# A graph layer with attention and experts: waiting aggregates as fp16 pairs, one layer as the loop body, and a reordered opening

## The chip, the core and the metric

The kernel runs on one core of a Trainium2 chip. The metric is the device time of one execution in microseconds (us), the median of several runs. TensorE is PE in the rows, VectorE is DVE, ScalarE is ACT, GpSimd is POOL and SyncE is SP.

## What is computed

The input is a node matrix x of 6250 rows by 512 columns and 100000 edges (src, dst), sorted by dst. After a layer norm of the rows the kernel adds a graph term and an attention term to x, then adds a mixture of two experts to the result.

```python
xn  = layernorm(x)
agg = segment_sum(xn[src], dst, 6250);  ah = agg / max(degree, 1)
gnn = xn @ W1.T + b1 + ah @ W2.T + b2
q, k, v = split(xn @ qkv_w.T); q, k = relu(q), relu(k)      # 16 heads of 32
p   = (q @ (k.T @ v)) / (q @ sum(k) + 1e-15)                # per head
x2  = x + gnn + p @ proj_w.T + proj_b
xn2 = layernorm(x2); pooled = sum(xn2 * softmax(xn2 @ attn_w))
g, (e1, e2) = top-2 gates of softmax(pooled @ gate_w + gate_b)
out = x2 + sum over the two experts of g * gelu(gelu(xn2 @ w1 + b1) @ w2 + b2)
```

## The kernel before, in words

The rows are cut into T = 49 tiles of 128. Precise values are carried as two fp16 halves (high and low), and `three` forms a product of such pairs with 12 matmuls of 128x512: high by high and high by low (L523, L524), then low by high (L526). Each engine has a program of its own, written out in order, and semaphores join them. There is no scheduler: the order in the source is the order on the engine, and a `Fori` is a loop on that engine.

**Pass 1** (iterations i = -1 to 49). ACT and DVE normalize tile n (`normalize(n)`: statistics L1073, L1074, scale L1059 to L1062, values L846 and L851, low half L1068), `LEAD` tiles ahead of PE and three in two iterations by `norm_slots`. SP stores the pair as a row block of `table` in DRAM. PE transposes tile i+1 (L658), which ACT copies into xT (L904), and turns a weight block in most of the early iterations (`prepare`, L569). It then computes the keys of tile i (L523 to L526), which ACT takes twice (L918, L920). The low half is made by POOL until i = KP = 28, afterwards by DVE (L1202), and PE adds the products of keys and rows of tile i-1 into four banks (L678 to L680). The first keys need the key weights: two loads, 16 transposes (L541), the largest entry (L1043), a matmul that spreads it over the partitions (L532), the high half on ACT (L895) and the low half on DVE (L1180).

**Gathers.** Once the table is stored, POOL issues 784 indirect DMAs (L496), each with the rows of 128 edges, into a ring of 16 slots, four slots for each release by PE. SP counts the landings and tells PE. These 784 instructions are written out one by one.

**Aggregates.** For a tile DVE builds one-hot matrices (`match`, L1125, L1131). PE multiplies them with the gathered rows, about 17 blocks in a tile (`agg_first`, `group`, `agg_last`: L583, L584, L586, L609, L639). Only three tiles are aggregated within pass 1 (`EARLY`), and one between the passes. When a tile is done DVE takes the degree and its reciprocal (`degrees`, L1139, L1142), and ACT scales the bank into one of four slots of `ah`, in fp32 (`keep_ah`, L887). There it waits for its layer.

**Pass 2** (`layer(i)`). Layer i computes queries of tile i, turns the aggregate (L735) and the attention input (L742) of tile i-1 and forms their linear products. It also aggregates tile i+skew, and normalizes and turns tile i-2 (L776). The skew is 2, then 1, then 0 (`LAYERS`). Since `ah` is indexed by a Python number k, the loop body holds four layers. The loops run over i = 4 to 15, 20 to 31 and 36 to 47, three turns each. The other layers are written out. After a turned aggregate ACT copies its high half (L954) and DVE makes the low half (L1293).

**Pass 3** computes the two experts in groups of four tiles.

Of the kernel before, what the change touches and what calls it, by code (L numbers as in the profile page):

```python
# [20 lines left out]
P = 128  # L21
# [23 lines left out]
LEAD = 6  # L45
# [63 lines left out]

def layers(eng, body):  # L110
# [12 lines left out]

def program(nc, x, src, dst, gw1, gb1, gw2, gb2, qkv_w, proj_w, proj_b, attn_w, attn_b, gate_w, gate_b,
            w1, b1, w2, b2, out):
    ctx = ExitStack()
    with ctx:
# [11 lines left out]
        def slots(first, n):  # L139
# [42 lines left out]
        k32, khl, kacc = work[:, 4], [work[:, 5 + b].bitcast(F16) for b in range(2)], work[:, 7]  # L182
        x2, xn2, acc, pT_, x_in, w32, xb, ahT_ = (work[:, k] for k in range(8))
        ah = work[:, 8:12]
# [76 lines left out]
        ps_o, ps_b, ps_ta, ps_tp, ps_tx = bank[1], bank[2], bank[3], bank[4], bank[0]  # L261
# [10 lines left out]
            turned_x2 agg_made dg_made rd_made ah_made ahT_hi ahT_lo pT_hi pT_lo lin_made xa_made x2_made x2_stored  # L272
# [16 lines left out]
        def natural(t):  # L289

            if t < T - NS:
                return xT[:, t + OFF].rearrange("p a n -> p (a n)")
            return (work[:, 10], work[:, 11], awb[:, :])[t - (T - NS)].bitcast(F16)
# [20 lines left out]
        def _(sp):  # L314
# [68 lines left out]
            with sp.Fori(0, passes) as a:  # L383
                with sp.Fori(0, ROUNDS) as g:
                    for k in range(R):
                        sp.wait_ge(slot_loaded[k], (a * ROUNDS + g) * 16 + 16)
                        if k % U == U - 1:
                            sp.sem_inc(s["arrived"], 1)
# [53 lines left out]
        def _(pool):  # L442
# [30 lines left out]
            for i in range(KP + 1):  # L473
# [7 lines left out]
                pool.tensor_tensor(out=khl[i % 2][:, D:2 * D], in0=k32, in1=khl[i % 2][:, 0:D],  # L481
# [35 lines left out]
        def _(pe):  # L517
# [132 lines left out]
            pe.sem_inc(s["oh_used"], OG)  # L650
            n = 0
            for i in range(-1, T + 1):
                t = i + 1
                if t < T:
                    pe.wait_ge(s["lo_made"], t + 1)
                    after(pe, s["t_taken"], t)
                    for q in range(2 * C):
                        r = nc.tensor.transpose(ps_t[:, q, :], natural(t)[:, q * P:(q + 1) * P], ident16[:])  # L658
                    r.then_inc(s["t_made"], 1)
# [3 lines left out]
                if 0 <= i < T:  # L663
                    pe.wait_ge(s["t_taken"], i + 1)
                    after(pe, s["k32_made"], i)
                    after(pe, s["khi_made"], i)
                    if i == 0:
                        pe.wait_ge(s["scales_made"], 1)
                        pe.wait_ge(s["wk_hi"], C)
                        pe.wait_ge(s["wk_lo"], C)  # L670
                    three(ps_k[:, :], lambda c: xT[:, i, c, :], lambda c: xT[:, i, C + c, :],
                          lambda c: wk[:, 0, c, :], lambda c: wk[:, 1, c, :], C).then_inc(s["k_made"], 1)
# [161 lines left out]
        def _(act):  # L834
            F = nc.scalar.activation

            for t in range(XI):
                act.dma_start(xin[:, t, :], x[t * P:(t + 1) * P, :]).then_inc(x_loaded[t], 16)
# [649 lines left out]
```

## Time and profile before

| what | value |
|---|---|
| runs, us | 1998.27, 1991.93, 2003.87 (median 1998.27) |
| the profiled execution | 2016.52 us, of which its span is 2013.7 us |
| granted TensorE clock, mean | 0.904 of full speed |
| PE busy | 1672.8 us, 83% of the span |
| DVE busy | 1055.3 us, 52% |
| ACT busy | 642.5 us, 32% |
| POOL busy | 841.4 us, 42% |
| pass 1, pass 2, pass 3 | to about 400 us, 440 to 1700 us, 1760 to 2014 us |

Busy time is the time in which an engine executes; the rest it waits or issues. The granted clock of 1.0 stands for 2.4 GHz and 0.5 for 1.2 GHz. In the rows a matmul's time is the time in which it is under way. Matmuls overlap, so the distance of their starts is what one costs.

### The profile page before, as it was taken

The numbers are of one execution on the slowest core, as the hardware profiler recorded it, in microseconds if no ns is written. First come the engines' busy times: TensorE is split into PE (matmuls) and PEld (weight loads), VectorE is DVE, ScalarE is ACT, GpSimd is POOL, SyncE is SP. The second block draws the span as 40 slices with busy tenths as digits, with TensorE's granted clock in tenths as the row PEclk, the third lists the DMA queues.
The fourth block names the chain that finished last, engine by engine and source line by source line (L and its number), as shares of the span: only waits on it lengthen the run. The fifth ranks groups of instructions, "written<-read, shape, count | busy, mean of one in ns | idle before, by whom it ended". The sixth has DMA issues, their size and how long they took to land.

```text
span 2013.7 us, 31010 instructions
## 1 busy us (share of the span) xinstructions
PE 1672.8 (83%) x8557; PEld 795.2 (39%) x8558; DVE 1055.3 (52%) x2199; ACT 642.5 (32%) x980; POOL 841.4 (42%) x867
## 2 busy tenths in 40 slices
PE   5999887788878878988888877887788878499997
PEld 3554333343434333433343333433334334244443
DVE  8665122144555444654555454744455545467667
ACT  6787322111222212312222221311222212355554
POOL 2444333335555555356555556355555552000000
PEclk9999898989988888988888888988898888699999
DMA  8433322335565565455655556456555553212232
GB/s 282 163 126 110 94 84 84 87 118 166 174 183 171 158 181 174 130 177 179 178 168 165 166 177 183 125 172 185 172 178 162 166 171 107 99 63 104 96 112 93
DMA packets 113596, 296.39 MB, mean 147 GB/s; under 512 B 18602, under 2 KB 21188, under 8 KB 113260
## 3 DMA queue, kind: packets, MB, share of 16 engines
q0 software_dynamic: 62720, 205.57, 35.1%
q1 hardware_dynamic: 35424, 60.21, 8.9%
q10 hardware_dynamic: 15372, 29.58, 4.2%
q8 instruction: 46, 0.75, 0.2%
q14 instruction: 34, 0.28, 0.0%
HBM read 255.80 MB, written 39.49 MB: 147 GB/s over the span
## 4 chain that ended last, share of the span: by engine, by line
PE 68%; issue 16%; DVE 4%; another core or an unknown queue 3%; ACT 2%; DVEq 0%; DMA 0%; ACTq 0%; SPq 0%
PE bank L523 15%; PE bank L524 14%; PE bank L526 14%; PE bank L583 9%; PE bank L584 8%; PE bank L776 1%; PE bank L678 1%; PE bank L679 1%; PE bank L680 1%; PE bank L742 1%; PE bank L735 1%; DVE ring L1432 1%; PE bank L658 0%; PE bank L586 0%
## 5 line engine op out<-in xcount | busy, mean ns | idle before, releaser
L496 POOL DMA_INDIRECT ring<-table,src_col x784 | 758.8, 968 | 710.8 <-PE bank L609 384.9
L583 PE MATMUL bank<-ring,onehot 128*128 x830 | 319.7, 385 | 59.5 <-issue 49.8
L584 PE MATMUL bank<-ring,onehot 128*128 x830 | 322.4, 388 | 43.0 <-issue 42.3
L1139 DVE TENSOR_SCALAR dg<-bank 128x1 f32<-128x1 f32 x49 | 7.7, 158 | 459.5 <-PE bank L639 206.5
L523 PE MATMUL bank<-wts,xT 128*128 128x512 f16 x588 | 229.7, 391 | 14.4 <-ACT work L920 11.2
L887 ACT ACTIVATE work<-bank,rd 128x512 f32<-128x512 f32 x49 | 33.7, 687 | 631.0 <-issue 360.0
L524 PE MATMUL bank<-wts,xT 128*128 128x512 f16 x588 | 229.8, 391 | 0.0
L523 PE MATMUL bank<-wts,work 128*128 128x512 f16 x392 | 181.6, 463 | 26.2 <-issue 25.7
L524 PE MATMUL bank<-wts,work 128*128 128x512 f16 x392 | 181.7, 464 | 14.1 <-issue 13.3
L1131 DVE TENSOR_TENSOR onehot<-iota_t,dst_col 128x512 f32 x244 | 169.0, 693 | 44.9 <-DVE iota_t L1125 24.6
L586 PE MATMUL bank<-ones,onehot 128*128 128x1 f16 x830 | 138.4, 167 | 43.1 <-issue 42.5
L526 PE MATMUL bank<-wts,xT 128*128 128x512 f16 x588 | 153.7, 384 | 1.5 <-issue 1.5
L526 PE MATMUL bank<-wts,work 128*128 128x512 f16 x392 | 119.9, 424 | 29.4 <-issue 29.0
L583 PEld LDWEIGHTS bank<-ring,onehot 128*128 x830 | 80.7, 97 | 152.0 <-issue 73.5
L586 PEld LDWEIGHTS bank<-ones,onehot 128*128 x830 | 80.9, 97 | 148.8 <-issue 62.2
L584 PEld LDWEIGHTS bank<-ring,onehot 128*128 x830 | 80.1, 96 | 63.1 <-issue 54.2
L945 ACT ACTIVATE xT<-bank 128x512 f32 (+1 forms) x49 | 29.2, 597 | 196.4 <-PE bank L776 111.1
L523 PEld LDWEIGHTS bank<-wts,xT 128*128 128x128 f16 (+1 forms) x588 | 58.7, 100 | 79.5 <-issue 22.0
L526 PEld LDWEIGHTS bank<-wts,xT 128*128 128x128 f16 (+1 forms) x588 | 58.5, 100 | 73.3 <-issue 6.6
L1006 ACT ACTIVATE work<-work 128x512 f32<-128x512 f32 x98 | 61.8, 630 | 80.2 <-DVE work L1442 79.1
L481 POOL TENSOR_TENSOR work<-work 128x512 f16<-128x512 f32 x29 | 34.0, 1171 | 127.7 <-ACT work L920 127.7
L524 PEld LDWEIGHTS bank<-wts,xT 128*128 128x128 f16 (+1 forms) x588 | 58.7, 100 | 57.2 <-issue 6.6
(259 smaller groups left out, 2800.2 us busy)
## 6 DMA issues: line engine op xcount, KB each, us to landing
ring<-table,src_col POOLq DMA_INDIRECT x784
x_rows<-work ACTq DMA_DIRECT2D x49, 256.0 KB
work<-in_x ACTq DMA_DIRECT2D x48, 256.0 KB
ring<-x_rows SPq DMA_DIRECT2D x12, 1024.0 KB, 5.3
out_x<-ring SPq DMA_DIRECT2D x12, 1024.0 KB
table<-xT SPq DMA_DIRECT2D x46, 256.0 KB, 2.0
ring<-in_x SPq DMA_DIRECT2D x42, 256.0 KB, 2.7
xT<-in_L_mix_qkv_weight SPq DMA_DIRECT2D x2, 1024.0 KB, 8.9
```

The source lines that it names most:

```text
L481: pool.tensor_tensor(out=khl[i % 2][:, D:2 * D], in0=k32, in1=khl[i % 2][:, 0:D], op=ALU.subtract).then_inc(s["klo_made"], 1)
L496: pool.indirect_dma_start(ring[:, n, :], None, table[:, :], bass.IndirectOffsetOnAxis(ap=ap, axis=0)).then_inc(slot_loaded[n], 16)
L523: mm(out_, wh(c), mh(c), start=first and c == 0, stop=False)
L524: mm(out_, wh(c), ml(c), start=False, stop=False)
L526: r = mm(out_, wl(c), mh(c), start=False, stop=last and c == n - 1)
L583: mm(ps_agg[:, :], w[:, k, :], rows[:, k, 0:D], start=start, stop=False, skip_group_check=True)
L584: r = mm(ps_agg[:, :], w[:, k, :], rows[:, k, D:2 * D], start=False, stop=stop, skip_group_check=True)
L586: d = mm(ps_deg[:, 0:1], w[:, k, :], ones16[:, 0:1], start=start, stop=False, skip_group_check=True)
L887: F(ah[:, k % SLOTS, :], ps_agg[:, :], ACT.Copy, scale=rd[:]).then_inc(s["ah_made"], 1)
L945: F(tile(t)[:, 0:C, :], ps_tx[:, :].rearrange("p (c n) -> p c n", c=C), ACT.Copy).then_inc(s["x2T_hi"], 1)
L1006: F(act2[:, j % 2, e], pre[:, j % 2, e], ACT.Gelu).then_inc(s["act_made"], 1)
L1131: V.tensor_tensor(onehot[:, bass.ds((q + t) % OG * U, U), :], iota_t[:, None, :].to_broadcast([P, U, P]), dst_col[:, bass.ds(q % GROUPS * ...
```

## The change

`ah` becomes a pair of fp16 halves. ACT writes the high half while it scales the bank (`ah_hi`), and DVE writes the low half straight from the bank (`ah_made`), at the end of `degrees`. PE then turns eight fp16 blocks instead of four fp32 blocks, ACT copies the turned pair in one instruction, and the DVE instruction L1293 is gone. The slot is indexed by a register. With that one layer is the body of the loops of pass 2, and they cover i = 4 to 16, 18 to 32 and 34 to 47. From i = 30 on pass 1 becomes loops too (`stretch`, `LATE`), cut where a tile is aggregated, and the first of these aggregates moves from i = 35 to i = 36. The gathers stay written out. In the opening `LEAD` falls from 6 to 3, `norm_slots` gives five tiles in three iterations, ACT issues two loads of x before the first statistics and four after, and DVE measures the key weights after the statistics of one tile.

```diff
-LEAD = 6
+LEAD = 3
-EARLY = {35: 0, 41: 1, 47: 2}
+EARLY = {36: 0, 41: 1, 47: 2}
+LATE = ((30, 37), (37, 42), (42, T - NS - 1))
-LAYERS = ((1, 2, None), (2, 16, 2), (16, 17, None), (17, 32, 1), (32, 33, None), (33, T, 0), (T, T + 3, None))
+LAYERS = ((1, 2, None), (2, 17, 2), (17, 18, None), (18, 33, 1), (33, 34, None), (34, T, 0), (T, T + 3, None))
 def norm_slots(i):
-    n = LEAD + (3 * (i + 1) + 1) // 2
-    return range(n, min(LEAD + (3 * (i + 2) + 1) // 2, T + 2))
+    n, m = (LEAD + (5 * k + 2) // 3 for k in (i + 1, i + 2))
+    return range(n, min(m, T + 2))
 def layers(eng, body):
     for lo, hi, skew in LAYERS:
-        a, b = min(max(-(-lo // SLOTS), 1), hi // SLOTS), hi // SLOTS
-        for i in range(lo, a * SLOTS if b > a else hi):
-            body(i, skew, i % SLOTS)
-        if b > a:
-            with eng.Fori(a, b) as g:
-                for k in range(SLOTS):
-                    body(g * SLOTS + k, skew, k)
-            for i in range(b * SLOTS, hi):
-                body(i, skew, i % SLOTS)
+        a, b = max(lo, 4), min(hi, T - 1)
+        if b - a < 2:
+            a = b = hi
+        for i in range(lo, a):
+            body(i, skew)
+        if a < b:
+            stretch(eng, lambda i: body(i, skew), a, b)
+        for i in range(b, hi):
+            body(i, skew)
...
+            def late(i):
+
+                turn_tile(i + 1)
+                key(i)
+                gram(i - 1)
+            for lo, hi in LATE:
+                stretch(pe, late, lo, hi)
+                if hi - 1 in EARLY:
+                    aggregate(EARLY[hi - 1])
...
-                    for c in range(C):
-                        r = nc.tensor.transpose(ps_ta[:, c * P:(c + 1) * P], ah[:, (k - 1) % SLOTS, c * P:(c + 1) * P], ident[:])
+                    for q in range(2 * C):
+                        r = nc.tensor.transpose(ps_ta[:, q, :], one(ah, t % SLOTS)[:, q * P:(q + 1) * P], ident16[:])
...
-                F(ah[:, k % SLOTS, :], ps_agg[:, :], ACT.Copy, scale=rd[:]).then_inc(s["ah_made"], 1)
+                F(one(ah, t % SLOTS)[:, 0:D], ps_agg[:, :], ACT.Copy, scale=rd[:]).then_inc(s["ah_hi"], 1)
...
             act.wait_ge(s["consts"], 2)
-            for n in range(LEAD - 1):
-                normalize(n)
+            normalize(0)
+            load_x(range(2, XI))
+            normalize(1)
...
                 V.reciprocal(rd[:], dg[:]).then_inc(s["rd_made"], 1)
+                after(dve, s["ah_hi"], t + 1)
+                a2 = one(ah, t % SLOTS)
+                V.scalar_tensor_tensor(out=a2[:, D:2 * D], in0=ps_agg[:, :], scalar=rd[:], in1=a2[:, 0:D],
+                                       op0=ALU.mult, op1=ALU.subtract).then_inc(s["ah_made"], 1)
...
-            for n in range(3):
-                normalize(n)
+            normalize(0)
             for h in range(2):
                 dve.wait_ge(wk_loaded[h], 16)
                 largest(raw_w[WK][:, 2 * h:2 * h + 2], 6 + h)
-                if h == 0:
-                    normalize(3)
...
-                    after(dve, s["ahT_hi"], t + 1)
-                    V.tensor_tensor(ahT[:, 1], ps_ta[:, :].rearrange("p (c n) -> p c n", c=C), ahT[:, 0],
-                                    ALU.subtract).then_inc(s["ahT_lo"], 1)
```

In the opening, ACT's program before had these instructions, from the fourth statistics to the first copied tile:

```order
L856 ACTIVATE std<-mv,epsc 128x1 [waits mv_made]
L846 ACTIVATE ring<-ring,nmr,rstd 128x512 [waits lo_made,nmr_made]
L851 ACTIVATE xT<-ring,nmr,rstd 128x512
L856 ACTIVATE std<-mv,epsc 128x1 [waits mv_made]
L895 ACTIVATE wts<-bank,scale 128x512 [waits wk_turned,scales_made]
L895 ACTIVATE wts<-bank,scale 128x512 [waits wk_turned] x3
L846 ACTIVATE ring<-ring,nmr,rstd 128x512 [waits lo_made,nmr_made]
L851 ACTIVATE xT<-ring,nmr,rstd 128x512
L856 ACTIVATE std<-mv,epsc 128x1 [waits mv_made]
L904 ACTIVATE xT<-bank 128x1024 [waits t_made]
```

Now it has these, from behind the first two loads to the same copy:

```order
L900 ACT_TABLE_LOAD [waits mv_made]
L900 ACTIVATE std<-mv,epsc 128x1 [waits consts]
L881 DMA ring<-in_x 128x512 x4
L890 ACTIVATE ring<-ring,nmr,rstd 128x512 [waits nmr_made]
L895 ACTIVATE xT<-ring,nmr,rstd 128x512
L900 ACTIVATE std<-mv,epsc 128x1 [waits mv_made]
L955 ACTIVATE wts<-bank,scale 128x512 [waits wk_turned,scales_made]
L955 ACTIVATE wts<-bank,scale 128x512 [waits wk_turned] x3
L890 ACTIVATE ring<-ring,nmr,rstd 128x512 [waits nmr_made]
L895 ACTIVATE xT<-ring,nmr,rstd 128x512
L900 ACTIVATE std<-mv,epsc 128x1 [waits mv_made]
L937 ACTIVATE xT<-bank 128x1024 [waits t_made]
```

The four scaled key blocks (`wts<-bank,scale`) stand behind two square roots and one normalized tile. Before, five square roots and four tiles stood ahead of them.

At the end of an aggregate, ahead of the one-hot matrices of the next tile, DVE's program before had these instructions (`first_i` holds the block numbers, which are loaded into registers):

```order
L1139 TENSOR_SCALAR dg<-bank 128x1 [waits agg_made]
L1142 RECIPROCAL rd<-dg 128x1 [waits ah_made,dg_made]
L1123 TENSOR_LOAD first_i
L1123 ISA x2
L1124 TENSOR_LOAD first_i
L1124 ISA x2
L1125 TENSOR_SCALAR iota_t<-iota,tile_base 128x128
```

Now it has these, at the same place:

```order
L1204 TENSOR_SCALAR dg<-bank 128x1 [waits agg_made]
L1207 RECIPROCAL rd<-dg 128x1 [waits ah_made,dg_made]
L1210 SCALAR_TENSOR_TENSOR work<-bank,rd,work 128x512 [waits ah_hi]
L1188 TENSOR_LOAD first_i
L1188 ISA x2
L1189 TENSOR_LOAD first_i
L1189 ISA x2
L1190 TENSOR_SCALAR iota_t<-iota,tile_base 128x128
```

One instruction of 128x512, which waits for ACT, now stands between the reciprocal and the next tile's register loads.

## Rows read from the trace of the kernel before

**Rows 1.** Stages: us, busy time (x instructions) of each engine, granted clock, DMA share, GB/s.

```profile
100.00:150.00 50.00, 49.46 (x300) 26.13 (x299) 34.82 (x89) 41.73 (x71) 22.48 (x18) 1.00 0.39 126
...
1000.00:1200.00 200.00, 161.15 (x812) 74.50 (x812) 98.96 (x214) 43.61 (x64) 113.37 (x118) 0.86 0.58 172
```

**Rows 2.** Timeline of the opening: start us, us, engine, line, what, [idle before <-releaser].

```profile
8.58 3.65 PE L541 MATMUL bank<-ident,xT 128*128 128x128 f32 x16 [4.96 <-DMA xT<-in_L_mix_qkv_weight]
...
18.14 0.77 PE L532 MATMUL bank<-ring,ones 128*128 128x128 f32 x2 [5.92 <-DVEq L1171]
...
21.38 2.42 ACT L895 ACTIVATE wts<-bank,scale 128x512 f16<-128x512 f32 x4 [0.89 <-DVEq L1176]
...
23.44 2.69 DVE L1180 SCALAR_TENSOR_TENSOR wts<-bank,scale,wts 128x512 f16<-128x512 f32 x4
...
25.27 1.03 ACT L904 ACTIVATE xT<-bank 128x1024 f16<-128x1024 f16 x1
...
28.11 0.63 PE L523 MATMUL bank<-wts,xT 128*128 128x512 f16 x1
...
49.82 0.67 PE L532 MATMUL bank<-ring,ones 128*128 128x256 f32 x2 [1.21 <-DVEq L1196]
```

**Rows 3.** Timeline of ACT, three copies of a turned tile in the steady part.

```profile
99.95 1.02 ACT L904 ACTIVATE xT<-bank 128x1024 f16<-128x1024 f16 x1 [1.43 <-PE bank L658]
...
106.43 1.03 ACT L904 ACTIVATE xT<-bank 128x1024 f16<-128x1024 f16 x1
...
112.52 1.02 ACT L904 ACTIVATE xT<-bank 128x1024 f16<-128x1024 f16 x1 [1.43 <-PE bank L658]
```

**Rows 4.** Timeline of pass 1's late part, PE and ACT.

```profile
221.69 0.61 PE L658 MATMUL bank<-ident,xT 128*128 128x128 f16 x8
...
231.88 1.02 ACT L904 ACTIVATE xT<-bank 128x1024 f16<-128x1024 f16 x1 [11.50 <-remote]
...
340.38 1.02 ACT L904 ACTIVATE xT<-bank 128x1024 f16<-128x1024 f16 x1 [8.90 <-remote]
...
400.87 0.60 ACT L918 ACTIVATE work<-bank 128x512 f32<-128x512 f32 x1 [6.72 <-remote]
```

**Rows 5.** Timeline of one layer and the start of the next.

```profile
1005.62 0.16 DVE L1139 TENSOR_SCALAR dg<-bank 128x1 f32<-128x1 f32 x1 [10.85 <-PE bank L639]
...
1006.01 0.69 ACT L887 ACTIVATE work<-bank,rd 128x512 f32<-128x512 f32 x1 [14.18 <-issue]
...
1008.22 2.86 DVE L1131 TENSOR_TENSOR onehot<-iota_t,dst_col 128x512 f32 x4 [0.63 <-DVE iota_t L1125]
...
1013.44 0.60 PE L735 MATMUL bank<-ident,work 128*128 128x128 f32 x4
...
1014.32 0.38 PE L583 MATMUL bank<-ring,onehot 128*128 x1
...
1016.58 0.94 POOL L496 DMA_INDIRECT ring<-table,src_col  x1 [6.86 <-PE bank L609]
...
1028.04 0.38 PE L583 MATMUL bank<-ring,onehot 128*128 x1 [1.02 <-issue]
...
1038.43 0.38 PE L523 MATMUL bank<-wts,xT 128*128 128x512 f16 x1
...
1041.02 0.60 PE L735 MATMUL bank<-ident,work 128*128 128x128 f32 x4
```

**Rows 6.** Timeline of POOL in an earlier layer.

```profile
539.32 0.94 POOL L496 DMA_INDIRECT ring<-table,src_col  x1 [5.38 <-PE bank L609]
...
551.10 0.94 POOL L496 DMA_INDIRECT ring<-table,src_col  x1 [1.91 <-remote]
```

**Rows 7.** Waits of DVE: us in total, times, longest us.

```profile
DVE iota_t L1125 <- issue: 60.3, 44, 1.9
```

**Rows 8.** DMA queues from 620 to 840 us: packets, MB, share of 16 engines.

```profile
q14 instruction: 1, 0.01, 0.0%
```

**Rows 9.** DMA queues from 850 to 1000 us, the same columns.

```profile
q8 instruction: 6, 0.10, 0.3%
```

More of the change, by code:

```diff
@@ L382, in _, with landed @@
             passes = sp.value_load(first_i[0:1, T + 1:T + 2], min_val=1, max_val=T)
[L383 to L388, printed above, removed]
+            def landed(it):
+                for k in range(R):
+                    sp.wait_ge(slot_loaded[k], it * 16 + 16)
+                    if k % U == U - 1:
+                        sp.sem_inc(s["arrived"], 1)
+            with sp.Fori(0, ROUNDS) as g:
+                landed(g)
+            with sp.If(passes > 1):
+                with sp.Fori(1, passes) as a:
+                    with sp.Fori(0, ROUNDS) as g:
+                        landed(a * ROUNDS + g)
             sp.wait_ge(s["chosen"], 1)
@@ L650, in _, with turn_tile, key, gram @@
             pe.sem_inc(s["oh_used"], OG)
-            n = 0
[L652 to L659, printed above, removed]
+            def turn_tile(t):
+                after(pe, s["t_taken"], t)
+                for q in range(2 * C):
+                    r = nc.tensor.transpose(ps_t[:, q, :], natural(t)[:, q * P:(q + 1) * P], ident16[:])
+                r.then_inc(s["t_made"], 1)
+            def key(t):
+                pe.wait_ge(s["t_taken"], t + 1)
+                after(pe, s["k32_made"], t)
+                after(pe, s["khi_made"], t)
+                three(ps_k[:, :], lambda c: tile(t)[:, c, :], lambda c: tile(t)[:, C + c, :],
+                      lambda c: wk[:, 0, c, :], lambda c: wk[:, 1, c, :], C).then_inc(s["k_made"], 1)
+            def gram(t, first=False, last=False):
+                pe.wait_ge(s["klo_made"], t + 1)
+                kh, kl = one(khl, t % 2)[:, 0:D], one(khl, t % 2)[:, D:2 * D]
+                for c in range(C):
+                    xh, xl = natural(t)[:, c * P:(c + 1) * P], natural(t)[:, D + c * P:D + (c + 1) * P]
+                    mm(bank[c][:, :], xh, kh, start=first, stop=False)
+                    mm(bank[c][:, :], xh, kl, start=False, stop=False)
+                    r = mm(bank[c][:, :], xl, kh, start=False, stop=last)
+                r.then_inc(s["g_made"], 1)
+            n = 0
+            for i in range(-1, LATE[0][0]):
+                pe.wait_ge(s["lo_made"], i + 2)
+                turn_tile(i + 1)
                 for kind, c in STEPS.get(i, ()):
@@ L682, in _ @@
+            for i in range(LATE[-1][1], T + 1):
+                if i + 1 < T:
+                    turn_tile(i + 1)
+                if i < T:
+                    key(i)
+                gram(i - 1, last=(i == T))
                 if i in EARLY:
-                    if EARLY[i] == 0:
-                        pe.wait_ge(s["steps_act"], STEPS_ALL)
-                        pe.wait_ge(s["steps_dve"], STEPS_ALL)
-                        pe.wait_ge(s["firsts_made"], 1)
                     aggregate(EARLY[i])
@@ L914, in _, with late @@
                 if i >= 0:
-                    act.wait_ge(s["k_made"], i + 1)
-                    after(act, s["klo_made"], i)
-                    after(act, s["kacc_made"], i)
-                    F(k32, ps_k[:, :], ACT.Relu, scale=SK).then_inc(s["k32_made"], 1)
-                    after(act, s["g_made"], i - 1)
-                    F(khl[i % 2][:, 0:D], ps_k[:, :], ACT.Relu, scale=SK).then_inc(s["khi_made"], 1)
+                    take_key(i)
+            for t in range(T - NS, T):
+                stored(act, t)
+            def late(i):
+                take_tile(i + 1)
+                take_key(i)
+            for lo, hi in LATE:
+                stretch(act, late, lo, hi)
+                if hi - 1 in EARLY:
+                    keep_ah(EARLY[hi - 1])
+            for i in range(LATE[-1][1], T):
+                if i + 1 < T:
+                    take_tile(i + 1)
+                take_key(i)
                 if i in EARLY:
-                    keep_ah(EARLY[i], EARLY[i])
+                    keep_ah(EARLY[i])
             act.wait_ge(s["pt_stored"], 16)
@@ L1176, in _ @@
             dve.sem_inc(s["scales_made"], 1)
[L1177 removed]
+            normalize(2)
             for c in range(C):
```

130 lines of the change are left out of this document (73 added, 57 removed).

## The prediction

> **What bounds the kernel now.** I read the stages first. From 100 to 150 us PE is busy for 49.46 of 50 us at full clock: pass 1 is bound by PE, and what ACT, DVE or POOL do there costs nothing unless PE then waits. From 1000 to 1200 us, in pass 2, PE is busy for 161.15 of 200 us, the granted clock is 0.86 (a mixture of 2.4 and 1.2 GHz), and no other engine is over 60% [rows 1]. So the two stages have different limits, and I read a timeline in each.
>
> Pass 2 takes most of the time. A layer lasts from one turned aggregate at 1013.44 to the next at 1041.02, 27.6 us [rows 5]. POOL starts a burst of gathers at 1016.58. Some 11 us into the burst PE begins to idle between its instructions, with no semaphore to blame: 1.02 us, put down to issue, at 1028.04 [rows 5]. In that stretch it starts about one instruction in 0.7 us for some 7 us, and runs at half clock for about as long after it. In an earlier layer the burst from 539.32 ends before that, and POOL's next one starts at 551.10 after a pause [rows 6]; there the layer lasts 20 us and PE has no such stretch. So a layer's length hangs on how long POOL gathers without a pause, and neither on ACT nor on DVE: ACT was idle for 14.18 us before it scaled the aggregate, DVE for 10.85 us before it took the degree [rows 5].
>
> The same shape shows three times in the late part of pass 1. ACT gets a copy's release late, after 11.50 us of idling at 231.88, 8.90 at 340.38 and 6.72 at 400.87 [rows 4]. The releaser is "remote", and PE had made the tile long before: the first of them ended its transposes at 221.69 + 0.61 = 222.30 [rows 4]. From there to 231.88 are 9.6 us; all three together make 9.6 + 8.9 + 6.7 = 25.2 us in which PE has nothing to do. They too begin some ten us after POOL began an unbroken burst.
>
> **The opening.** Before, the 16 transposes of the key weights are done at 8.58 + 3.65 = 12.23, but the matmul that spreads the largest entry starts only at 18.14, and ACT scales the high half at 21.38, since DVE and ACT normalize tiles in between [rows 2]. Now one tile stands ahead of the measurement on DVE, so PE's matmul can follow its transposes at about 12.3. From 18.14 to 21.38 are 3.24 us, of which DVE spends 0.9 on a tile's statistics; without them the high half starts at about 14.5, 6.9 us earlier. The low half ended at 23.44 + 2.69 = 26.13, 4.75 us after the high half began [rows 2]; a tile's normalization stands between them, for which I allow 0.9 more: 20.1. The first keys followed ACT's copy of tile 0 by 28.11 - 25.27 = 2.84 us [rows 2]. With the copy now behind one tile of ACT's (some 2 us after the high half ends at 16.9) that would give 22; DVE reaches the low half of tile 1 later than it did, so I take 23.5 to 24, a gain of 4.3. It isn't all kept. The matmul for the next scale stands at 49.82, after an idle time of 1.21 that DVE caused [rows 2]. DVE's work ahead of it is the same in sum, so I expect it at 48.9, or 45 if PE alone set it. The gain carried on is 1.4 to 5; I take **-3 us**. Four of the loads of x are issued behind ACT's first square root; a late one would move the second or third tile only.
>
> **The pattern of normalized tiles.** ACT's copies are 106.43 - 99.95 = 6.48 us apart across an iteration with two tiles, and 112.52 - 106.43 = 6.09 across one with one [rows 3]; ahead of the second copy ACT shows no idle time, so there ACT is as late as PE. Now two iterations of three have two tiles, where one of two had. If each added double costs 6.48 - 6.09 = 0.39, the bound is 30/6 x 0.39 = 2 us for the thirty iterations, less what the fewer iterations with norms give back. If ACT fell behind in each of 20 doubles it would be 20 x 0.39 = 8. I take **+1.2 us**: the copy at 106.43 was released without a wait, nearer to the small end.
>
> **The late part as loops.** PE's, ACT's and DVE's instructions are the same, and one aggregate moves from behind i = 35 to behind i = 36. What the loops save is code. Whether the three late releases go with it is a rival below. My value is **0**: they follow POOL's burst, and POOL's gathers stay as they are.
>
> **The layers.** Hidden, each:
> - DVE's new low half: one of 128x512 from a bank, like the one of 23.44 (2.69 / 4 = 0.67 us each [rows 2]), and ahead of it a wait for ACT's 0.69 us [rows 5]. Behind it on DVE stand the next tile's one-hot matrices. They would start at about 1008.22 + 0.9 = 1009.1, and the first four be done by 1012, where PE takes its first block at 1014.32 [rows 5]. The cover is 14.32 - 11.08 = 3.2 us; without it this edit would cost 0.9 us x 46 = 41 us.
> - The removed subtraction on DVE took as long and had the same cover: 0.
> - Eight fp16 transposes took 0.61 us in pass 1 [rows 4], four fp32 ones 0.60 [rows 5]: 0.
> - ACT's copy takes 1.02 us [rows 3] where it took about 0.6, with 14.18 us of idle time to spend [rows 5].
>
> **Loop turns.** There were 9 turns of loops in pass 2 and are 13 + 15 + 14 = 42. One lies ahead of the query at 1038.43, where i passes from 23 to 24, and PE shows no idle time there [rows 5]. DVE shows 60.3 us before L1125 in 44 times, 1.37 on average, and 1.9 at the longest [rows 7]; if the excess of 0.5 is the turn, 33 more cost 33 x 0.5 = 17.5 us on DVE, and nothing on PE as long as the 3.2 us above stand. I take **0**.
>
> **The sum** is -3 + 1.2 + 0 + 0 = -1.8 us. The profiled execution took 2016.52 us, 18 more than the median of 1998.27; a change of this size is carried over as it stands: **1996 us**.
>
> **A rule against the change.** The DMA queues show that code is fetched while the program advances: from 850 to 1000 us, mostly written-out layers, the queue of instructions moved six blocks [rows 9], and from 620 to 840, in the later turns of a loop, one queue moved a single packet and the other none [rows 8]. Layers take 27 to 28 us in both stretches. So neither fetching nor its absence costs anything that I can see. The Trainium skill ("Runtime: NRT & Kernel Launch", section "Instruction fetch mechanics") says that a taken branch whose target lies outside a window of two pages waits for a fetch, and that kernels therefore unroll; its blocks of 16 KiB agree with 0.10 MB for six. By it loops of four layers would pay at each turn and loops of one might not. The trace has no fetch at the turns of either kind of loop to show it.
>
> **Rivals.**
> - *The late releases come from written-out code.* ACT's three late releases lie where PE fetched code; in loops it doesn't. For it: they are put down to "remote", and no engine was busy. Against it: they last 7 to 10 us, the layers show the same in a loop and outside one, and bursts of POOL lead all of them. It gives 1996 - 25 = **1971**. Chance 0.20.
> - *PE's stretch of slow issue in the layers comes from the length of the loop body*, and a body of one layer ends it. A layer would last 20 us as in the stretch of [rows 6], some 7 less, for 46 layers less four that have none: about 1996 - 42 x 7 = **1700**. Against it: written-out layers and loops are alike. Chance 0.03.
> - *Slower: the turn of a loop is exposed on PE's path.* It is DVE's turn that matters: the price is 17.5 us as above if the one-hot matrices arrive late, which needs 3.2 us of delay at the start of a tile where I count 0.9 + 0.5. Layers with a tile of 18 blocks come nearest. It gives 1996 + 17.5 = **2013.5**. Chance 0.17.
> - *My forecast*: 0.60. Its own range is 1988 to 2006: the opening at -5 or -1.4 and the pattern at +8 or 0 give -5 to +6.6, and runs scatter by 6 about their median.
>
> **How the numbers follow.** What a measurement here can tell from no change is about 0.5%, 10 us: faster is under 1988.3, slower over 2008.3. Of my forecast's 0.60, 0.06 lies under the one and 0.03 over the other. Faster is then 0.20 + 0.03 + 0.06 = 0.29. Slower is 0.17, of which 0.02 lies within the bound, and 0.03: 0.18. The rest, 0.53, is the same. The range goes from 1968, under the first rival, to 2016, over the last; only the 1700 is left out, with tails of each.
>
> **What the profile will show.** Right: the first keys at 23.5 to 24, the spreading matmul of the second scale at about 49; in the late part ACT waits three times for 6 to 12 us with "remote" named; layers of 27 to 28 us, PE idle "issue" some 11 us into POOL's burst; clock about 0.86 in the middle of pass 2; DVE's new instruction at 0.67 to 0.75 us and one-hot matrices done over 2 us before their first block. Wrong: a late part without the three waits (first rival); layers of 20 us (second); idle time on PE before a tile's first block that a one-hot matrix ends (third). A cost that I can't see is what a shorter body does to the burst itself: if POOL's gathers are released in another rhythm, each layer's slow stretch could move by more than all terms above.

## The result, and the profile after

The changed kernel took 2032.77 us (median of 4 runs, 2023.00 to 2036.49), the kernel before 1997.84 us (4 runs, 1991.93 to 2003.87). The ratio is 1.0167, with an interval from 1.0119 to 1.0215: slower by 35 us. Forecast were 1996 us and a range up to 2016. The profiled execution of the changed kernel took 2030.38 us. A ratio, here and below, leaves out executions that are over 1.5% above the fastest of their kernel, while a median holds them all (pause_8: 1.0042 by medians, 1.0004 as ratio).

Its stages, with the columns of [rows 1]:

```profile
0.00:25.00 25.00, 11.57 (x68) 8.83 (x69) 20.50 (x62) 13.95 (x23) 4.30 (x23) 0.86 0.81 273
25.00:50.00 25.00, 17.35 (x82) 8.07 (x81) 18.90 (x35) 16.00 (x28) 7.58 (x6) 0.85 0.72 237
50.00:75.00 25.00, 24.77 (x140) 12.66 (x138) 15.39 (x48) 18.61 (x34) 7.60 (x6) 0.94 0.63 187
...
100.00:150.00 50.00, 47.31 (x288) 24.94 (x286) 34.50 (x90) 40.15 (x68) 23.07 (x18) 1.00 0.40 127
1000.00:1200.00 200.00, 162.57 (x853) 75.56 (x854) 104.93 (x221) 47.91 (x67) 112.86 (x117) 0.87 0.58 169
```

Pass 2 reads as before. Pass 1 doesn't: from 100 to 150 us PE is busy for 47.31 us where it was for 49.46 [rows 1], and from 25 to 50 us its granted clock is 0.85 (1.00 before). The timeline of the changed kernel, PE in the opening and ACT in the late part:

```profile
20.82 0.63 PE L538 MATMUL bank<-wts,xT 128*128 128x512 f16 x1
...
29.70 0.58 PE L538 MATMUL bank<-wts,xT 128*128 128x512 f16 x1 [4.44 <-ACT work L946]
...
48.16 0.67 PE L547 MATMUL bank<-ring,ones 128*128 128x256 f32 x2 [3.21 <-DVEq L1271]
...
229.37 0.60 ACT L944 ACTIVATE work<-bank 128x512 f32<-128x512 f32 x1 [4.53 <-remote]
...
240.96 1.02 ACT L937 ACTIVATE xT<-bank 128x1024 f16 x1 [10.51 <-remote]
...
355.05 1.02 ACT L937 ACTIVATE xT<-bank 128x1024 f16 x1 [7.59 <-remote]
...
413.55 0.60 ACT L944 ACTIVATE work<-bank 128x512 f32<-128x512 f32 x1 [6.01 <-remote]
```

The first keys come at 20.82 us, 7.3 us earlier than at 28.11 [rows 2]. The next keys then wait 4.44 us for ACT, and the spreading matmul of the second scale 3.21 us for DVE. The late releases are still there, as before the change [rows 4].

A good ruler is the start of ACT's copy of the keys of tile i (L918 before, L944 after), since it stands once in every iteration, and then the turned aggregate of layers 0 and 48 (L735 before, L776 after). All times are us in the profiled execution:

| kernel | i = 4 | i = 28 | layer 0 | i = 28 to layer 0 | layers 0 to 48 |
|---|---|---|---|---|---|
| before | 59.74 | 208.04 | 441.13 | 233.1 | 1258.4 |
| changed, first profile | 59.23 | 214.24 | 455.99 | 241.7 | 1258.4 |
| changed, second profile | 57.58 | 214.31 | 460.11 | 245.8 | 1272.7 |

By layer 0 the first profile of the changed kernel is 14.9 us behind: 6.2 by i = 28, 8.7 from there on. The layers cost nothing in the first profile and 14 us in the second. One execution of a kernel differs from another by more than the term that was forecast for them. The medians are 35 us apart and these two profiled executions only 14 (2030.38 and 2016.52), since the one of before lies 18 us above its median; the profiles alone don't show where the rest is.

### The profile page after: what moved, and what is told of

Its sections match the earlier page's. It is cut to its first block, busy times and chain, and to the rows that moved or that the text cites. A ratio compares the mean times of both kernels' runs of the same rounds, so it can differ in the third digit from the quotient of the medians.

```text
span 2028.6 us, 33311 instructions
## 1 busy us (share of the span) xinstructions
PE 1688.6 (83%) x8753; PEld 798.8 (39%) x8754; DVE 1060.8 (52%) x2199; ACT 663.9 (33%) x980; POOL 837.9 (41%) x867
## 4 chain that ended last, share of the span: by engine, by line
PE 43%; issue 26%; DVE 9%; DVEq 5%; ACT 5%; another core or an unknown queue 4%; ACTq 1%; DMA 0%; SPq 0%
PE bank L538 10%; PE bank L539 10%; PE bank L541 9%; PE bank L598 5%; PE bank L599 4%; DVEq L1196 1%; PE bank L687 1%; PE bank L689 1%; PE bank L688 1%; ACT work L1019 1%; DVE work L1360 1%; DVE work L1357 1%; DVE st L1363 1%; DVEq L1189 1%
## 5 line engine op out<-in xcount | busy, mean ns | idle before, releaser
L931 ACT ACTIVATE work<-bank,rd 128x512 f32 (+1 forms) x49 | 33.7, 688 | 576.9 <-issue 331.3
L538 PEld LDWEIGHTS bank<-wts,xT 128*128 (+1 forms) x588 | 58.5, 100 | 87.5 <-issue 29.5
L538 PEld LDWEIGHTS bank<-wts,work 128*128 128x128 f16 x392 | 43.0, 110 | 124.4 <-issue 97.5
L541 PEld LDWEIGHTS bank<-wts,xT 128*128 (+1 forms) x588 | 58.7, 100 | 73.7 <-issue 7.7
```

Source lines behind the costliest of these rows:

```text
L538: mm(out_, wh(c), mh(c), start=first and c == 0, stop=False)
L541: r = mm(out_, wl(c), mh(c), start=False, stop=last and c == n - 1)
L931: F(one(ah, t % SLOTS)[:, 0:D], ps_agg[:, :], ACT.Copy, scale=rd[:]).then_inc(s["ah_hi"], 1)
```

## The experiments

An experiment on one edit takes it alone to the kernel before, or takes it alone out of the changed kernel. They ran in five sessions, each with its own runs of the kernel before. These gave 1672.8, 2012.9, 1996.9, 1998.5 and 1672.3 us: in two sessions every kernel was a sixth faster, on the same program. Ratios hold within a session. I call the sessions of 1670 us quick and those of 2000 us slow; the last section shows the difference.

| kernel | session | us | ratio to before, interval |
|---|---|---|---|
| again | quick | 1670.02 | 0.9983, 0.9970 to 0.9996 |
| old_opening | quick | 1679.33 | 1.0031, 1.0019 to 1.0044 |
| flat_late | quick | 1682.45 | 1.0046, 1.0026 to 1.0066 |
| pattern_3_in_2 | quick | 1670.75 | 0.9983, 0.9972 to 0.9995 |
| changed | slow | 2047.69 | 1.0167, 1.0137 to 1.0198 |
| opening_alone | slow | 2004.36 | 0.9952, 0.9926 to 0.9978 |
| pairs_alone | slow | 2027.59 | 1.0077, 1.0047 to 1.0107 |
| pause_8 | slow | 2021.31 | 1.0004, 0.9970 to 1.0038 |
| flat_late_2 | slow | 2027.68 | 1.0144, 1.0111 to 1.0177 |
| pattern_again | slow | 2021.26 | 1.0125, 1.0090 to 1.0160 |
| four_layers | slow | 2022.76 | 1.0131, 1.0099 to 1.0163 |
| opening_pause | slow | 1892.40 | 0.9449, 0.9409 to 0.9488 |
| dve_once_more | slow | 2007.97 | 1.0040, 1.0012 to 1.0068 |
| pairs_opening_pause | slow | 1959.30 | 0.9690, 0.9607 to 0.9774 |
| opening_pause_4 | slow | 1892.45 | 0.9478, 0.9416 to 0.9540 |
| four_layers_pause | slow | 1992.72 | 0.9885, 0.9804 to 0.9966 |
| pairs_alone_2 | quick | 1676.48 | 1.0025, 1.0012 to 1.0038 |
| pause_4_alone | quick | 1791.55 | 1.0706, 1.0681 to 1.0731 |

**again** is the kernel before, unedited.

> The kernel before once more, for a second profile: the one shown took 2016.5 us, 18 above the median. Theory 1 (the change costs in the opening, in the pattern of normalized tiles and in the late part, and nothing in the layers): its layers last 27 to 28 us each like those of both profiles, and pass 1 ends up to 18 us earlier than the profile shown (the copy for the last key by 383 to 401 us), because one or two of the three late releases are missing. Theory 2 (the layers became slower too): pass 1 ends where it did, and the time that the median is shorter lies in the layers. Time 1992 to 2004 us.

It fell into a quick session, so it couldn't answer. It gave a floor instead: the same program differs from itself by 0.17%, 3 us. flat_late, pattern_3_in_2 and old_opening fell into the same session, without the changed kernel beside them, so their forecasts in us weren't tested either.

**changed** is the changed kernel, unedited.

> The changed kernel itself, beside its parts. If this chip gives the kernel before in about 1998 us, it takes 2033 us; if it gives it in about 1670 us, theory 1 (it is the written-out form without its gain or loss: the pattern's double iteration at i = 0 and what it does to the clock, then the aggregates of the late part) says 1680 to 1684 us, a ratio of 1.004 to 1.007; the rival (the loops of the late part cost 10 us or more beside that) says 1692 us or more.

The ratio of 1.0167 came again, to the last digit, in a session in which both kernels took 15 us longer.

**opening_alone**, the first edit taken to the kernel before:

```diff
-LEAD = 6
+LEAD = 3
+            load_x(range(2))
...
-            for n in range(LEAD - 1):
-                normalize(n)
+            normalize(0)
+            load_x(range(2, XI))
+            normalize(1)
```

> The kernel before with the new opening alone (LEAD 3, loads of x in two parts, the key weights measured after one tile); three tiles in two iterations as before, everything written out, aggregates in fp32. Theory 1: the keys of i = 3 and of i = 28 are back 7 to 8 us earlier than before, and the kernel gains as much, a ratio of 0.995 to 0.996. Rival (an earlier opening only makes PE idle and halves its clock, so that nothing is carried on): 1.000.

Theory 1 holds: the copy for i = 28 starts at 200.79 us instead of 208.04, and the kernel gains 9 us. The spreading matmul of the second scale starts 7.5 us earlier than before, at 42.28 us where the changed kernel has it at 48.16:

```profile
42.28 0.67 PE L532 MATMUL bank<-ring,ones 128*128 128x256 f32 x2
```

**pattern_3_in_2** and **pattern_again** are one kernel, the changed one with the old pattern:

```diff
-LATE = ((30, 37), (37, 42), (42, T - NS - 1))
+LATE = ((32, 37), (37, 42), (42, T - NS - 1))
-    n, m = (LEAD + (5 * k + 2) // 3 for k in (i + 1, i + 2))
+    n = LEAD + (3 * (i + 1) + 1) // 2
```

> The changed kernel with its own opening, but three tiles in two iterations as before; the loops of the late part begin two iterations later, since the last tiles are normalized by then. Theory 1 (two of three double iterations make PE wait 0.3 to 0.8 us for ACT, against 0.3 in every second): it gains 3 to 5 us on the changed kernel, 2029 us. Rival (the clock lost in the opening is the whole cost): no gain, 2033 us.

> Three tiles in two iterations with the rest of the changed kernel, once more. By the copies of the keys (200.5 against 214.2 us for i = 28) it is 13.7 us faster than the changed kernel: a ratio of 1.009 to 1.011 on a chip with 2000 us; if it is 1.016, something later takes the gain back. On a chip that takes 1670 us: 0.998 as before.

The copy for i = 28 starts at 200.58 us where the changed kernel's started at 214.31: the pattern cost 13.7 us, in kernels with the new opening (with the old one it wasn't tried). PE's second keys in pattern_again and its spreading matmul, then its windows:

```profile
27.29 0.38 PE L538 MATMUL bank<-wts,xT 128*128 128x512 f16 x1 [2.00 <-ACT work L946]
...
41.63 0.67 PE L547 MATMUL bank<-ring,ones 128*128 128x256 f32 x2 [0.36 <-DVEq L1271]
```

```profile
25.00:50.00 25.00, 21.31 (x121) 10.82 (x120) 22.90 (x47) 19.93 (x35) 9.72 (x8) 1.00 0.82 272
...
100.00:150.00 50.00, 49.21 (x298) 26.04 (x297) 35.72 (x91) 41.69 (x72) 23.43 (x18) 1.00 0.38 127
```

The pattern of five in three puts two tiles into i = 0 where the other has one, and again into i = 2. After the first, ACT's keys are 2.4 us later, and PE idles 4.44 us instead of 2.00. After the second, the spreading matmul waits 3.21 us for DVE instead of 0.36. The granted clock from 25 to 50 us is 0.85 instead of 1.00. By the copy for i = 4 (51.55 us in pattern_again) that is 6.0 us against the second profile of the changed kernel and 7.7 against the first. The other 6 to 8 come in the 24 iterations behind it (47.31 against 49.21 us of PE's work in 50). PE's waits for ACT's keys from 60 to 200 us (us, times, longest), in the changed kernel and in pattern_again:

```profile
PE bank L538 <- ACT work L946: 8.2, 11, 2.0
```

```profile
PE bank L538 <- ACT work L946: 4.6, 10, 0.8
```

So ACT is the engine that PE waits for more there. In the time of the whole kernel 8.5 us show, less than the 11 to 15 that the expectation wanted, and the intervals overlap; in the quick session it was 12 us against flat_late, which has the pattern of five in three and differs in the late part besides.

**old_opening**, the changed kernel with LEAD = 6, the pattern and the opening of before:

> The changed kernel with the opening of before: LEAD 6, three tiles in two iterations, the six loads and the five square roots ahead of the key weights. Theory 1: the keys of i = 28 are back at 208 us from 214.2 and the kernel gains 6 us on the changed one: 2027 us. Theory 2 (the loops of the late part and the layers cost it all): no gain, 2033 us. Theory 3 (the shift of the table sets where the gathers fall and with it the late releases): back by 15 us or more, under 2018 us.

It has the copy for i = 28 at 208.71 us, where the kernel before has it (208.04). It lies 9 us above pattern_3_in_2 in the same session, which is what the new opening is worth with the old pattern.

**flat_late** and **flat_late_2**, the late part written out:

```diff
+    if (lo, hi) in LATE:
+        for i in range(lo, hi):
+            body(i)
+        return
     with eng.Fori(lo, hi) as i:
```

> The changed kernel with the late part of pass 1 written out on PE, ACT and DVE as before, the aggregates where the change puts them. Theory 1 as the profiles have it (late releases in both forms, of 25 us in all in either): within 5 us of the changed kernel, 2028 to 2038 us. Rival (a loop in the late part costs some 6 to 20 us: the turns, or releases that come late in loops more often): 2013 to 2027 us.

> The late part written out, once more, for a chip on which the kernel before takes about 2000 us. Theory 1 (the pattern costs 13.5 us, the pairs 15, the opening gives back 7 to 8, and what is left to 35, some 13 us, is the loops of the late part): 12 us or more faster than the changed kernel, a ratio to before of 1.008 to 1.011. Rival (the 13 us belong to the layers, one as the body): 1.015 to 1.018. On a chip that takes 1670 us: 1.0046 as before.

flat_late_2 is 4.6 us faster than the changed kernel by the ratios, less than the intervals can tell from nothing. The expected 12 us or more didn't come; the ratio of 1.0144 lies next to the rival's 1.015 to 1.018. From i = 28 to layer 0 it takes 239.3 us. The four profiles of slow sessions that aggregate behind i = 35 take 231 to 234 us there, and the five without a pause that do so behind i = 36 take 238 to 246, in loops or not. So the loops aren't needed for that loss. Whether the shift by one iteration is its cause wasn't tried by itself.

**four_layers**, the changed kernel with the loops of before:

```diff
+            with eng.Fori(a, b) as g:
+                for k in range(SLOTS):
+                    body(g * SLOTS + k, skew)
```

> The changed kernel with loops whose body is four layers, over i = 4 to 15, 20 to 31 and 36 to 47 as before; the rest as changed. Theory 1 (a body of one layer costs nothing): as the changed kernel, 1.0165. Rival (42 turns of a loop cost PE or DVE 5 to 15 us): 1.009 to 1.014.

Its 1.0131 points to 7 us for a body of one layer, again within the intervals of both. Layers 0 to 48 take 1255.0 us.

**pairs_alone** and **pairs_alone_2**, fp16 pairs taken to the kernel before:

```diff
-                        r = nc.tensor.transpose(ps_ta[:, c * P:(c + 1) * P], ah[:, (k - 1) % SLOTS, c * P:(c + 1) * P], ident[:])
+                        r = nc.tensor.transpose(ps_ta[:, q, :], ah[:, (k - 1) % SLOTS, q * P:(q + 1) * P], ident16[:])
...
+                after(dve, s["ah_hi"], t + 1)
+                V.scalar_tensor_tensor(out=a2[:, D:2 * D], in0=ps_agg[:, :], scalar=rd[:], in1=a2[:, 0:D],
```

> The kernel before with fp16 pairs alone: ACT's high half and DVE's low half at the end of an aggregate, eight fp16 transposes, one copy. Loop bodies of four layers, everything else as before. My prediction: nothing, 1.000. Theory 1: the layers stay as they are and the three early aggregates and the stretch up to layer 1 lose 3 to 6 us, a ratio of 1.002 to 1.004. Rival (the loops, and not the pairs, lose that): 1.000.

> The kernel before with fp16 pairs alone, a second time, since its first profile was the lowest of its executions (2015.7 us at a median of 2027.6). Theory 1 (the pairs cost something): a ratio of 1.005 to 1.010 again, and a profile near its median, in which the loss of 10 to 15 us against the kernel before shows between the copy for the last key and the last layer. Rival (chance): 0.998 to 1.003.

The pairs cost 14.7 us in a slow session (9 to 22 by the interval) and 4.2 in a quick one, little more than the 3 us by which a program there differs from itself. One place shows in every profile of a kernel with pairs. It is `degrees(SKEW)` between the passes, in the timeline of pairs_alone_2:

```profile
401.32 0.70 ACT L888 ACTIVATE work<-bank,rd 128x512 f16<-128x512 f32 x1
...
402.06 0.75 DVE L1146 SCALAR_TENSOR_TENSOR work<-bank,rd,work 128x512 f16<-128x512 f32 x1 [2.61 <-ACT work L888]
402.72 2.72 DVE L1266 SCALAR_TENSOR_TENSOR wts<-bank,kscale,wts 128x512 f16<-128x512 f32 x4
403.61 0.63 PE L743 MATMUL bank<-ident,work 128*128 128x128 f32 x4 [2.28 <-DVE wts L1266]
```

ACT scales four blocks of the mixing matrix ahead of the aggregate. DVE's new instruction waits for the aggregate, 2.61 us, and the four low halves of the matrix (L1266) stand behind it, and PE behind those. In the profile of again DVE began them at once:

```profile
396.05 2.73 DVE L1261 SCALAR_TENSOR_TENSOR wts<-bank,kscale,wts 128x512 f16<-128x512 f32 x4 [0.30 <-ACT wts L938]
...
396.59 0.60 PE L735 MATMUL bank<-ident,work 128*128 128x128 f32 x4
397.03 0.60 PE L742 MATMUL bank<-ident,work 128*128 128x128 f32 x4
```

From layer 0 to layer 1 are 13.83 us with pairs and 11.29 without; in slow sessions it is 17.67 (pairs_alone) against 14.53 (before). The rest of the 14.7 us isn't found: the profile of pairs_alone, the fastest of its executions (2015.66 us), has the same 1258.4 us for layers 0 to 48 as the one of before.

A second place was suspected, the layer behind a short one. The kernel before, and then the changed kernel, at the start of layer 28's blocks:

```profile
1172.98 0.39 PE L583 MATMUL bank<-ring,onehot 128*128 x1 [0.72 <-DVE onehot L1131]
```

```profile
1192.33 0.39 PE L598 MATMUL bank<-ring,onehot 128*128 x1 [2.00 <-DVE onehot L1196]
...
1194.05 0.60 PE L598 MATMUL bank<-ring,onehot 128*128 x1 [0.71 <-DVE onehot L1196]
```

Both layers ahead are short (20.3 and 19.3 us instead of 27), the blocks are due some 7 us sooner, and DVE is late already in the kernel before, so the cover of 3.2 us isn't there. The sums in the view of waits, of before and of the changed kernel (us, times, longest):

```profile
PE bank L583 <- DVE onehot L1131: 9.3, 8, 2.4
```

```profile
PE bank L598 <- DVE onehot L1196: 17.8, 13, 2.8
```

That these waits come with the pairs isn't shown: pairs_alone has 12.2 us in all, 5.2 of them from 440 to 1720 us where before has 2.5, and in the quick session it is 6.7 with pairs and 7.0 without.

**dve_once_more** has that place on DVE and fp32 aggregates:

```diff
+                after(dve, s["ah_hi"], t + 1)
+                V.tensor_scalar(ah[:, k % SLOTS, :], ps_agg[:, :], rd[:], None, ALU.mult).then_inc(s["ah_made"], 1)
```

> The kernel before, aggregates in fp32, but at the end of degrees DVE waits for ACT's scaled aggregate and writes the same values over it once more, and only that signals ah_made: the place and the length of the new instruction without the pairs. Theory 1 (fp16 pairs cost 15 us because the next tile's one-hot matrices stand behind that wait on DVE): a ratio of 1.006 to 1.010 where the pairs gave 1.0077. Rival (the eight fp16 transposes or the longer copy cost it): 1.000 to 1.002.

1.0040 lies between the theories. The place on DVE costs something by itself, some 8 us (2 to 14 by the interval). 3.3 of them are at `degrees(SKEW)` again: from layer 0 to layer 1 are 17.88 us instead of 14.53, with the same wait on DVE and PE behind it:

```profile
444.95 0.75 DVE L1144 TENSOR_SCALAR work<-bank,rd 128x512 f32<-128x512 f32 x1 [2.61 <-issue]
...
446.50 1.09 PE L742 MATMUL bank<-ident,work 128*128 128x128 f32 x4 [3.85 <-issue]
```

PE's waits for one-hot matrices are 8.0 us, no more than before, so theory 1's reason, the matrices that stand behind the new wait, doesn't show here. Whether the rest of the pairs' 15 is the transposes, the copy or chance stays open.

**pause_8** and the kernels below give POOL a pause of ten chained memsets after every eighth gather:

```diff
                 fetch(b % R, src_col[:, b:b + 1])
+                if b % 8 == 7:
+                    for k in range(10):
+                        after(pool, s["paused"], b // 8 * 10 + k)
+                        pool.memset(idx_slots[:], 0).then_inc(s["paused"], 1)
```

> The changed kernel, with ten chained memsets of 16 numbers on POOL after every eighth gather, 2 to 3 us of POOL's time without a gather. On a chip where layers take 27 us: if PE's slow stretch hangs on more than eight gathers in a row, it is gone or shorter, layers take 20 to 22 us and the kernel 1750 to 1900 us; if not, layers stay at 27 us and the kernel at 2033 us. On a chip where layers take 20 us, POOL with 17 gathers of 1.25 us has no room for it: layers of 22 to 24 us, 1780 us.

> The kernel before with the new opening and with the pause of POOL after every eighth gather: the two edits that gained. On a chip with 2000 us: the opening gives 0.995 and the pause took 26 us from the changed kernel, together 0.980 to 0.985; if the pause only repaired what the change broke (the late part), 0.995. On a chip with 1670 us the pause costs more than the opening gives, over 1.01.

> As the version that took 0.945, with half the pause after every fourth gather in place of a whole one after every eighth: the same POOL time, shorter bursts. If the length of a burst sets PE's slow stretch, 0.90 to 0.94; if only the sum of pauses does, 0.945; if a pause of 1 us is too short to end it, 0.97 or more.

> The kernel before with half a pause of POOL after every fourth gather and nothing else, to part the pause from the opening. The opening alone gave 0.9952 and both together 0.948: 0.952 to 0.955 if they add. On a chip with 1670 us: 1.01 or more, since POOL has no time to give away there.

The pause, in POOL's timeline of opening_pause, takes 1.65 us:

```profile
1024.32 1.16 POOL L496 DMA_INDIRECT ring<-table,src_col  x1 [0.30 <-issue]
1025.47 1.65 POOL L506 MEMSET idx_slots<- 128x16 int32 x10
1027.27 0.95 POOL L496 DMA_INDIRECT ring<-table,src_col  x1
```

On the changed kernel the pause takes the ratio from 1.0167 to 1.0004, and the 1750 to 1900 us that were expected if the slow stretches ended didn't come. On the kernel with the new opening alone it does more: with it that kernel takes 104.5 us less than the kernel before in a slow session (1996.94 - 1892.40); the opening alone took 8.6. A layer's mean goes from 26.1 us (opening_alone, 1251.1 / 48) to 24.7 (1184.4 / 48), and layer 0 comes at 401.07 us instead of 431.48. PE's idle time put down to issue (no releaser shows) falls from 228 us in the whole profile of opening_alone to 149. So PE's slow stretches and the late releases do hang on POOL's gathers, but they are shortened and not ended: layers still take 20 to 33 us, and one release is still 6.8 us late. Half a pause twice as often does the same (0.9478), which points to the sum of the pauses and not to the length of a burst; 0.90 to 0.94 was expected if the length counted. The executions of the kernels with a pause scatter by up to 3% (1861.02 to 1916.98 us for this last one). In a quick session the pause on the kernel before costs 7%. It is no better version, then, but one that depends on the session. The pause without the new opening never ran in a slow session.

> The kernel before with the new opening, the pause after every eighth gather, and fp16 pairs; loop bodies of four layers, the late part written out. Without the pairs the ratio was 0.945. Theory A (what keeps the pause from helping the changed kernel is the pairs, whose instruction holds back the one-hot matrices): 0.98 or more. Theory B (it is the loop body or the late loops): 0.95 to 0.96.

> The changed kernel with loop bodies of four layers and the pause after every eighth gather. The changed kernel with the pause gave 1.0004. Theory A (the pairs): 0.995 to 1.00, hardly better. Theory B (the one-layer body keeps the pause from helping): 0.96 or less.

With pairs added the 0.9449 becomes 0.9690, and with the four-layer body the changed kernel's 1.0004 becomes 0.9885. Neither theory is the whole: pairs and the one-layer body both keep part of the pause's gain away, the second by intervals that nearly touch (0.9966 and 0.9970).

## Why the prediction was wrong

Two of its steps failed by more than the runs leave open: the pattern, taken at +1.2 us, and the pairs, taken at 0.

**What bounds the kernel**: right in the main. Pass 1 is bound by PE, and the slow stretches hang on POOL's gathers, which the pause has shown. That a layer's length hangs on how long a burst goes on unbroken isn't borne out by opening_pause_4. The half clock behind a slow stretch lasts 5 us in the timeline before (1032.97 to 1038.4), not 7.

**The opening**: right in direction, too small in size. The first keys came at 20.82 us, forecast were 23.5 to 24. The spreading matmul of the second scale came at 48.16 and forecast was 48.9, but that is luck: the opening alone brings it to 42.28, and the pattern puts it back. "DVE's work ahead of it is the same in sum" was the error, since a lower `LEAD` leaves fewer tiles to normalize ahead of it: three fewer with the old pattern, two with the new. Taken alone it carries 7.2 us into the steady part (208.04 - 200.79), where "1.4 to 5; I take -3 us" stood.

**The pattern** is the first step that failed: "I take +1.2 us: the copy at 106.43 was released without a wait, nearer to the small end". It cost 13.7 us by i = 28, 6 to 8 of them by i = 4, where PE isn't yet supplied, and 8.5 us of the whole time. I had counted iterations of the steady part alone, and 0.39 us for each; there it cost 6 to 8 us, with single waits of up to 2.0. The copy without idle time was read the wrong way round: it means that ACT had nothing left to give, and the end of the range at 8 us was the likelier one. With the opening's 7.2 us this makes +6.5, where -1.8 stood for both; 6.3 were measured (214.31 - 208.04).

**The late part**: "My value is 0" failed as well. Late releases stayed, so the first rival fell. But the part took 5 to 13 us more (238 to 246 us against 233), of which the loops themselves are at most a part. The 9.6 us of the first late release were also misread: PE still had keys and products to do until 227.5 us, and then idled 5.57 and 3.39 us, 9.0 in sum. The size was right by luck.

**The layers, "Hidden, each"**, is the second step that failed, and by the ratios the larger one: the pairs cost 14.7 us in a slow session and 4.2 in a quick one. The place on DVE alone cost 8. The cover of 3.2 us was read from one layer between two long ones. Behind a short layer it is below zero, though no run shows what that costs. `degrees(SKEW)`, which cost 3.1 to 3.4 us, wasn't looked at: a wait on an engine was added, and what is queued behind it there are four halves of a weight, not one-hot matrices. Where the other 11 us go is open.

**Loop turns**: the third rival, slower at 2013.5 us, had the right side, but its cause isn't shown. PE's waits for one-hot matrices doubled (9.3 to 17.8 us), but four_layers, with 9 turns instead of 42, still has 17.3 of them, so the turns aren't needed for it. What four_layers gained on the changed kernel, 7 us, is within the intervals.

**The sums**: 33 x 0.5 is 16.5; the 17.5 is 33 times the unrounded 0.53. The forecast's own range ends too low: its +6.6 and the scatter of 6 reach 2011 us, not 2006. Neither would have covered 2033.

On code, the page of the profile of the changed kernel has this row of the queues, where the kernel before had 46 packets:

```profile
q8 instruction: 26, 0.43, 0.1%
```

So less code was fetched, and the kernel was slower: no time was won by fetching less. The rule weighed in the prediction (the Trainium skill, "Runtime: NRT & Kernel Launch", section "Instruction fetch mechanics": a taken branch out of the window waits for a fetch) would make the shorter body the better one. No run shows that: 1.0131 with four layers in the body, 1.0167 with one.

By the ratios of slow sessions, the pairs are +0.77%, the pattern +0.42, the body +0.36, the late loops +0.23, the opening -0.48: 1.30%, where 1.67 were measured with intervals of 0.3 each. The parts come from different sessions. The pairs carry the most, then the pattern; the two smaller ones aren't told from nothing. By ratios alone the pattern isn't either (its interval overlaps the changed kernel's), but its 13.7 us stand in the rows.

## What to carry to other kernels

Read the cover of an inserted wait (the time by which its engine may be late without another one waiting) at its worst use: the shortest iteration, and each place outside the loop where the helper is called, with what is queued behind it there. A schedule that is harmless in the steady state can be dear in its first iterations, where an idle PE also loses its clock. And where one execution differs from the next by 15 us, a second profile of the kernel before is worth more than a finer sum on the first.

## What the runs showed of the hardware

I hadn't expected that the same program runs in 2000 or in 1672 us, session by session. The stages from 1000 to 1200 us of opening_alone and opening_pause (slow), and again and pause_4_alone (quick), each from its own profile:

```profile
1000.00:1200.00 200.00, 166.08 (x857) 77.44 (x856) 105.75 (x227) 47.40 (x70) 110.84 (x116) 0.88 0.58 169
```

```profile
1000.00:1200.00 200.00, 167.93 (x877) 79.08 (x875) 109.47 (x238) 50.53 (x74) 127.49 (x253) 0.94 0.58 170
```

```profile
1000.00:1200.00 200.00, 194.23 (x1120) 97.68 (x1119) 140.13 (x302) 63.66 (x95) 145.10 (x148) 1.00 0.74 221
```

```profile
1000.00:1200.00 200.00, 172.59 (x975) 85.71 (x973) 120.88 (x262) 54.50 (x80) 148.82 (x291) 0.99 0.67 196
```

In again (quick) PE's idle time put down to issue is 42 us in all, where it is 243 in before (slow). The granted clock from 1000 to 1200 us is 1.00, most layers take 19.5 to 22 us instead of 27 to 28, and the late part has none of the late releases. POOL's share of the time is 73% there (145.10 of 200 us), so it has none to give to a pause. In a slow session a gather takes no longer (0.97 us on average in opening_alone, 0.99 in again), yet PE falls behind once some nine have gone out in a row (from 1016.58 to the idle time ahead of 1028.04 [rows 5]). What differs between the sessions, these runs don't show. One slow and one quick session ran on the same chip.

The clock fell behind idle time that was short. In the changed kernel PE idled 4.44 us ahead of 29.70; its matmul then took 0.58 us, the next ones 0.63, and the granted clock from 30 to 34 us was 0.50, which is 1.2 GHz. After 2.00 us of idling in pattern_again the matmul took 0.38 us and the clock stayed at 1.00. In flat_late_2, with the changed kernel's pattern, PE idled 3.40 us there and the clock from 30 to 34 us was still 1.00; its copy for i = 4 starts at 55.70 us, earlier than the 57.58 and 59.23 of the changed kernel. So one and the same schedule loses the clock in one execution and keeps it in another. A wait's price on PE is therefore the wait and what the clock takes after it.
